# Attention scores in PSUM: the row maxima on a ring of four banks, the scores on two

## The reference, cut to what matters

```
q, k, v = heads(x @ Wq), heads(x @ Wk), heads(x @ Wv)        # 16 heads, D = 32
attn = softmax(q k^T / sqrt(D));  std = (attn v) @ Wo
qa, ka = affinities(q), affinities(k)                        # to 8 splats per head
w = qa amp ka^T;  w = w / (sum_k w + 1e-8);  dgsa = (w v) @ Wo
out = (1 - blend) std + blend dgsa
```

## Time and profile before

| what | value |
|---|---|
| median of 3 runs | 1607.84 us (1604.98 to 1620.33) |
| the profiled execution | 1618.21 us, of which the span of its trace is 1616.0 us |
| mean granted clock of PE | 0.846 of full speed |
| busy: PE, DVE, ACT, POOL | 76%, 75%, 46%, 16% of the span |
| matmul instructions, DVE instructions | 4597, 1425 |

### The profile page before, as it was taken

How to read it: one execution, slowest core, us unless ns; L and a number is a source line. 1 busy time by engine, 2 the same in 40 slices (tenths; PEclk the granted TensorE clock), 3 DMA queues, 4 the chain that set the end, 5 groups by cost and what they waited for, 6 DMA issues and landing times.

```text
span 1616.0 us, 14035 instructions
## 1 busy us (share of the span) xinstructions
PE 1224.5 (76%) x4597; PEld 573.4 (35%) x4602; DVE 1214.8 (75%) x1425; ACT 744.4 (46%) x1102; POOL 257.9 (16%) x299
## 2 busy tenths in 40 slices
PE   5664747777788857788888867778888867786895
PEld 4332212323444422233444422223444422232453
DVE  5968979789648986889547986889648985889423
ACT  6674425443376424444365524444376423443231
POOL 1000222001112221001112231001112221011111
PEclk8766978879899978789799978789799977889798
DMA  6853894655249793555259694555258694455253
GB/s 199 268 165 99 187 217 110 128 118 116 81 119 216 167 225 108 121 114 130 54 132 221 144 220 117 113 121 127 57 134 204 154 216 115 99 127 114 61 141 97
DMA packets 116759, 228.54 MB, mean 141 GB/s; under 512 B 14560, under 2 KB 25312, under 8 KB 116688
## 3 DMA queue, kind: packets, MB, share of 16 engines
q1 hardware_dynamic: 89248, 144.95, 31.6%
q0 software_dynamic: 26496, 81.80, 26.7%
q10 hardware_dynamic: 944, 0.92, 0.2%
HBM read 116.08 MB, written 29.62 MB: 90 GB/s over the span
## 4 chain that ended last, share of the span: by engine, by line
DVE 31%; PE 31%; DMA 14%; issue 7%; ACT 4%; SPq 2%; POOL 1%; DVEq 0%; ACTq 0%; POOLq 0%
PE ps L1420 12%; DVE ST L844 10%; PE ps L1390 6%; DMA qk_parts<-PT 5%; DVE ST L836 5%; DVE MX L900 4%; PE ps L1228 4%; DMA GU<-gu_tiles 4%; PE ps L1245 3%; DVE ST L847 3%; DVE BST L880 2%; DMA KS<-qk_parts 2%; DMA YA<-ST 2%; SPq L343 2%; PE ps L1334 1%
## 5 line engine op out<-in xcount | busy, mean ns | idle before, releaser
L844 DVE TENSOR_TENSOR_SCAN ST<-dA,ST 128x1024 f32<-128x1024 f32 x128 | 316.6, 2473 | 15.3 <-ACT dA L546 11.8
L1420 PE MATMUL ps<-V,GU 128*128 128x512 f16 x1024 | 251.3, 403 | 25.0 <-DMA GU<-gu_tiles 19.4
L1228 PE MATMUL ps<-KS,QS 96*128 96x512 f32 x256 | 135.8, 610 | 149.5 <-DVE MX L900 80.4
L900 DVE TENSOR_REDUCE MX<-ps 128x1 f32<-128x512 f32 x256 | 164.9, 686 | 107.0 <-PE ps L1228 107.0
L447 POOL DMA_DIRECT2D YA<-ST x128 | 109.6, 856 | 819.6 <-DVE ST L847 793.6
L546 ACT ACTIVATE dA<-DL,Aneg 128x511 f32<-128x511 f32 x256 | 168.8, 713 | 95.5 <-DVE ST L844 95.3
L677 ACT ACTIVATE PT<-ps 128x1024 f32<-128x1024 f32 x128 | 125.0, 1019 | 118.7 <-PE ps L1334 118.0
L836 DVE TENSOR_TENSOR ST<-DU,BC 128x1024 f32<-128x1024 f32 x128 | 155.9, 1218 | 12.7 <-DMA BC<-bc_rows 7.9
L847 DVE TENSOR_TENSOR ST<-ST,BC 128x1024 f32<-128x1024 f32 x128 | 159.4, 1245 | 4.4
L1420 PEld LDWEIGHTS ps<-V,GU 128*128 128x128 bf16 x1024 | 100.3, 103 | 169.7 <-issue 42.3
L1390 PE MATMUL ps<-WP,QS 128*128 128x512 f32 x512 | 145.6, 429 | 14.2 <-DVE QS L1033 13.0
(11 more groups left out here) (224 smaller groups left out, 1627.8 us busy)
## 6 DMA issues: line engine op xcount, KB each, us to landing
YA<-ST POOLq DMA_DIRECT2D x128, 512.0 KB, 7.3
BC<-bc_rows SPq DMA_DIRECT2D x64, 512.0 KB, 5.6
qk_parts<-PT SPq DMA_DIRECT2D x64, 256.0 KB, 6.6
GU<-gu_tiles SPq DMA_DIRECT2D x64, 256.0 KB, 3.5
WP<-proj_tiles SPq DMA_DIRECT2D x64, 256.0 KB, 2.8
QS<-qk_parts SPq DMA_DIRECT2D x48, 256.0 KB, 5.3
KS<-qk_parts SPq DMA_DIRECT2D x48, 256.0 KB, 6.0
RD<-PT POOLq DMA_DIRECT2D x28, 256.0 KB, 4.9
```

The lines of the kernel that those rows point to most:

```text
L844: nc.vector.tensor_tensor_scan(flat, dA[:, a, :, :].rearrange("p e s -> p (e s)"), flat, 0.0, ALU.mult, ALU.add).then_inc(s_scan, 1)
L900: nc.vector.tensor_reduce(MX[:, j % 2, qt, h:h + 1], ps[:, n % 2, :], AX_X, ALU.max).then_inc(s_mx, 1)
L1228: mm(ps[:, n % 2, :], QS[i][0:3 * D, h, qt * P:(qt + 1) * P], KS[i][0:3 * D, h, :], start=True, stop=True).then_inc(s_xs, 1)
L1420: last = mm(ps[:, f % F_RING, :], GU[:, t % 2, k, m * P:(m + 1) * P], XHL[:, z, k, :], start=(k == 0 and z == 0), stop=(k == KT - 1 and z ...
```

## The change

Three things move together.

1. The max tiles get a ring of four banks, 0 to 3, from tile n = 20 of each batch on. The first 20 tiles (those of group 0, and the four of group 1 that come ahead of the stage) stay on banks 0 and 1. A tile waits for the reduction of the tile that had its bank before.
2. Both score pairs use banks 4 and 5, so pair s waits for the exponential of pair s - 1. PE's order in a quarter changes with it: before it was pair 0, tiles, pair 1, tiles, values bank 6, tiles, values bank 7, tiles; now it is pair 0, tiles, values bank 6, tiles, pair 1, tiles, values bank 7, tiles. In quarter 0 of groups 1 to 3 no tile stands between the pairs.
3. The splat transposes and the key-value product move to bank 3 (SPARE_BANK). The wait for ACT's copy stands at the first tile of group 2 in bank 3, and the wait for `splat_kv` at the first tile of group 3 in bank 3, which is tile 2 (n = 50). The denominator product moves behind pair 1 of its quarter.

```diff
+        MAX_TILES = KT * HG
+        def max_bank(j, m):
+            n = MAX_TILES * j + m
+            return n % 2 if n < MAX_TILES + X_AHEAD else (n + 1) % 4
+        def max_bank_before(j, m):
+            n = MAX_TILES * j + m
+            same = [q for q in range(n) if max_bank(*divmod(q, MAX_TILES)) == max_bank(j, m)]
+            return same[-1] if same else None
+        def first_in_bank(j, m):
+            return all(max_bank(j, q) != max_bank(j, m) for q in range(m))
+        SPARE_BANK = 3
...
-                        nc.scalar.copy(QAK[:, 2, :], ps[:, 1, :]).then_inc(s_ka, 1)
+                        nc.scalar.copy(QAK[:, 2, :], ps[:, SPARE_BANK, :]).then_inc(s_ka, 1)
...
-                            nc.scalar.activation(PT[:, kt % 2, 2 * p:2 * p + 2, :], ps[:, 2 + 2 * p:4 + 2 * p, :],
+                            nc.scalar.activation(PT[:, kt % 2, 2 * p:2 * p + 2, :], ps[:, 4:6, :],
...
-                    nc.vector.tensor_reduce(MX[:, j % 2, qt, h:h + 1], ps[:, n % 2, :], AX_X, ALU.max).then_inc(s_mx, 1)
+                    nc.vector.tensor_reduce(MX[:, j % 2, qt, h:h + 1], ps[:, max_bank(j, i), :], AX_X, ALU.max).then_inc(s_mx, 1)
...
-                    if n >= 2:
-                        pe.wait_ge(s_mx, 16 * NG * b + n - 1)
-                    if j > 0 and m == 0:
+                    bank, before = max_bank(j, m), max_bank_before(j, m)
+                    if before is not None:
+                        pe.wait_ge(s_mx, 16 * NG * b + before + 1)
+                    if j > 0 and bank == 0 and first_in_bank(j, m):
                         since(pe, s_br, NG * b + j)
-                    if j == 2 and m == 1:
+                    if j == 2 and bank == SPARE_BANK and first_in_bank(j, m):
                         pe.wait_ge(s_ka, b + 1)
-                    mm(ps[:, n % 2, :], QS[i][0:3 * D, h, qt * P:(qt + 1) * P], KS[i][0:3 * D, h, :],
+                    if j == KV_GROUP + 1 and bank == SPARE_BANK and first_in_bank(j, m):
+                        pe.wait_ge(s_kvm, 4 * b + 4)
+                    mm(ps[:, bank, :], QS[i][0:3 * D, h, qt * P:(qt + 1) * P], KS[i][0:3 * D, h, :],
...
-                        steps = (0, 0, 4, 4) if j > 0 and kt == 0 else (0, 2, 4, 6)
+                        steps = (0, 0, 0, 4) if j > 0 and kt == 0 else (0, 2, 4, 6)
                         cuts = [min(tiles[0] + n, tiles[1]) for n in steps] + [tiles[1]]
                         for p in range(2):
                             s = 2 * (KT * j + kt) + p
-                            if s < 2:
+                            if s == 0:
                                 pe.wait_ge(s_dist, 2 * (b + 1))
                                 pe.wait_ge(s_pj2, 2 * (b + 1))
                             else:
-                                pe.wait_ge(s_exp, 2 * KT * NG * b + s - 1)
+                                pe.wait_ge(s_exp, 2 * KT * NG * b + s)
...
-                                last = mm(ps[:, 2 + h, :], KS[i][0:3 * D + 1, h, kt * P:(kt + 1) * P],
+                                last = mm(ps[:, 4 + h % 2, :], KS[i][0:3 * D + 1, h, kt * P:(kt + 1) * P],
...
-                                pe.wait_ge(s_kvm, 4 * b + 4)
-                            max_scores(b, j + 1, cuts[p], cuts[p + 1])
-                        if j == NG - 1 and kt == 0:
-
-                            pe.wait_ge(s_br, NG * (b + 1))
-                            pe.wait_ge(s_kvm, 4 * b + 3)
-                            mm(ps[:, 0, :], QAK[:, 4, 0:P], QAK[:, 0, :], start=True, stop=True).then_inc(s_den, 1)
-                        for p in range(2):
+                            max_scores(b, j + 1, cuts[2 * p], cuts[2 * p + 1])
+                            if j == NG - 1 and kt == 0 and p == 1:
+
+                                pe.wait_ge(s_br, NG * (b + 1))
+                                pe.wait_ge(s_kvm, 4 * b + 3)
+                                mm(ps[:, 0, :], QAK[:, 4, 0:P], QAK[:, 0, :], start=True, stop=True).then_inc(s_den, 1)
                             if kt > 0:
                                 values(b, j, kt - 1, 6 + p)
-                            max_scores(b, j + 1, cuts[2 + p], cuts[3 + p])
+                            max_scores(b, j + 1, cuts[2 * p + 1], cuts[2 * p + 2])
```

More of the change, by code:

```diff
@@ L947, in splat_kv @@
                 dve.wait_ge(s_kv, b + 1)
-                nc.vector.scalar_tensor_tensor(out=QAK[:, 3, :], in0=ps[:, 1, :], scalar=par[:, AMP:AMP + 1], in1=mask,
+                nc.vector.scalar_tensor_tensor(out=QAK[:, 3, :], in0=ps[:, SPARE_BANK, :], scalar=par[:, AMP:AMP + 1], in1=mask,
                                                op0=ALU.mult, op1=ALU.mult).then_inc(s_kvm, 1)
@@ L1340, in attention_phase @@
                                 for k in range(KT):
-                                    last = mm(ps[:, 1, :], QAK[:, 2, k * P:(k + 1) * P], V[:, k, :], start=(k == 0), stop=(k == KT - 1))
+                                    last = mm(ps[:, SPARE_BANK, :], QAK[:, 2, k * P:(k + 1) * P], V[:, k, :],
+                                              start=(k == 0), stop=(k == KT - 1))
                                 last.then_inc(s_kv, 1)
-                                pe.wait_ge(s_kvm, 4 * b + 4)
-                            max_scores(b, j + 1, cuts[p], cuts[p + 1])
-                        if j == NG - 1 and kt == 0:
-                            pe.wait_ge(s_br, NG * (b + 1))
-                            pe.wait_ge(s_kvm, 4 * b + 3)
-                            mm(ps[:, 0, :], QAK[:, 4, 0:P], QAK[:, 0, :], start=True, stop=True).then_inc(s_den, 1)
-                        for p in range(2):
+                            max_scores(b, j + 1, cuts[2 * p], cuts[2 * p + 1])
[3 more added lines that the diff above has]
+                                mm(ps[:, 0, :], QAK[:, 4, 0:P], QAK[:, 0, :], start=True, stop=True).then_inc(s_den, 1)
                             if kt > 0:
                                 values(b, j, kt - 1, 6 + p)
-                            max_scores(b, j + 1, cuts[2 + p], cuts[3 + p])
+                            max_scores(b, j + 1, cuts[2 * p + 1], cuts[2 * p + 2])
                         if j + 1 < NG and kt == KT - 2:
@@ L1366, in attention_phase @@
                         for k in range(KT):
-                            last = nc.tensor.transpose(ps[:, 1, k * P:(k + 1) * P], QAK[:, 1, k * P:(k + 1) * P], ident[:, :])
+                            last = nc.tensor.transpose(ps[:, SPARE_BANK, k * P:(k + 1) * P], QAK[:, 1, k * P:(k + 1) * P], ident[:, :])
                         last.then_inc(s_kat, 1)
```

## The result

The changed kernel took **1632.51 us** (median of 4 runs, 1625.71 to 1637.67), the kernel before on the same chip 1607.19 us (4 runs, 1604.98 to 1620.33). The ratio on record is 1.0128, with a 95% interval of 1.0093 to 1.0164; the quotient of these two medians is a little larger, 1.0158. I had forecast 1604.4 us and a range of 1584 to 1620 us, so the result lies above the range.

What follows compares the result with a forecast made beforehand. A stage was taken as a chain alternating DVE's maxima with PE's tiles and the link through the stack load. Terms -13.4 - 11.6 + 10.4 + 4.1 + 3.6 + 3.45 = -3.5 us gave 1604.4 us, range 1584 to 1620.

Steps and rivals of the forecast that it cites:

- Group 1: Max tiles of group 1: four banks remove 3.35 of DVE's 4.67 us idle time per batch, 13.4 us over four batches.
- Group 2: Max tiles of group 2: four banks remove 2.9 us of DVE's idle time per batch, 11.6 us over four batches.
- rival A: PE's clock rises early in groups 1 and 2 without bank stalls, and costs hide: 1585 us; chance 0.20.
- Load of the stack: Group 0 to 1: the last score pair releases SP's load 2.0 us later; 2.6 us a batch, 10.4 us lost in all.
- From group 1 to 2: Last maximum of group 1 to first of group 2: 14.55 us in the changed kernel, 4.1 us lost in all.
- T0: Start of the transposes, put 0.1 us after the last maximum in the changed kernel.
- Landing: Stack load's DMA time from issue to arrival: taken as 10.3 us, near the lower of 9.73 and 11.74 us.
- Rival B: Stack load bounds: each us of landing beyond 10.3 costs 8 us, giving 1616 to 1624 us; chance 0.14.
- Hidden behind DVE's three halves: Group 3: some 0.7 us more per quarter on ACT and PE costs nothing; only the late denominator costs, 3.45 us.
- Group 0: Score pairs no longer run ahead, so tile 8 reaches DVE late: 0.9 us, 3.6 us lost in all.
- the splat product is late: Group 1 to 2: DVE gets `splat_kv` at 13.1 us where ready at 11.4, hidden unless the landing takes under 9.5 us.
- what would show it: Profile signs: DVE's idle time falls from 107.0 to about 80 us, with 4.5 to 5 us ahead of group 1's first maximum.

Runs made afterwards that it cites:

- experiment 5: Changed kernel, but in the last quarter of groups 0 and 1 POOL issues the YA additions only after the stack load has landed; 1615.56 us, ratio 1.0029.
- experiment 6: Changed kernel, but SP issues the last quarter's BC loads in groups 0 and 1 only after the stack has landed; 1629.29 us, ratio 1.0112.
- experiment 4: Kernel before, but SP issues the stack load only after the group's last exponential has ended; 1645.3 us, ratio 1.0214.
- Experiment 2: Changed kernel, but all of group 3 has pair 1 on banks 2 and 3 and the old PE order; 1624.86 us, ratio 1.0082.
- experiment 1: Changed kernel, but the last quarter of groups 0 to 2 has pair 1 on banks 2 and 3 and the old order; 1593.34 us, ratio 0.9878.
- experiment 11: Kernel before, with only the last quarter's score pairs moved ahead of the transposes; 1599.63 us, ratio 0.9932.
- experiment 10: Kernel before's banks, new PE order in quarters 1 and 2 of groups 1 and 2, last quarter's score pairs ahead of the transposes; 1592.86 us, ratio 0.9903.
- experiment 7: Changed kernel, with the max tiles of all groups back on banks 0 and 1; 1662.75 us, ratio 1.0312.
- experiment 9: Kernel before's banks, with only the new PE order in quarters 1 and 2 of groups 1 and 2; 1606.7 us, ratio 0.9961.

## Why the prediction was wrong

**The gains were right or too small.** Group 1 gained 13.9 us for 13.4, by the walk that I had made: the halves of quarter 1 start 10.4 us after the landing (1036.93 against 1026.56 us), forecast 10.3, and quarter 2 has no gap. Group 2 gained 21.1 us for 11.6. The term was mis-sized because I walked through it at the clock of before; it was granted 0.86 to 0.95. This is rival A's mechanism, in one of its two groups. Group 1 stayed at 0.64 to 0.69. The Trainium skill ("TensorE: Matmul & The Clock Gate", "A second HAM failure mode: psum-queue depth-cycling") reports of another kernel that its clock went up and down as it cycled through PSUM banks. Here the ring of four is in place in both groups, and the clock was no lower than before in either (0.64 to 0.69 for 0.58 to 0.68 in group 1).

**The step that failed is "Load of the stack"**, and with it the term "From group 1 to 2". I forecast 14.5 us for both ways together and they cost 37.3. (The four differences behind the 4.1 us add up to 4.0.) Split by the eight loads, 20.9 us are later issues and 16.2 us slower landings (0.2 are left).

- *Issue.* I took 2.0 us more per load and it was 2.6, up to 3.6 in group 0. I had the last pair end at T0 + 3.65 us, in every load, with a pair's duration at the full clock. Two things held it up. In group 0 of batches 1 to 3 it was ACT's order: I had ended the first exponential at T0 + 3.1 us, from the ACT rows of the old order. With one pair at a time, quarter 2's last exponential ended later; the four dA exponentials of the next halves and the bias row stand behind it in ACT's order, and the exponential that releases the last pair stands behind those (the chain above). It ended at T0 + 3.9 (1014.40 against 1010.52 us), and SP issued 4.7 to 5.2 us after T0. In the other five loads ACT stood idle ahead of the bias row, so its order held nothing. In three of those (group 0 of batch 0, group 1 of batches 2 and 3) PE had the low clock there, 0.50 to 0.56, and SP issued 4.6 to 4.9 us after T0; in the last two, at a clock of 0.96 and 1.00, 3.8 to 3.9 us, near the forecast. Batch 2, group 1 (T0 is 1045.37 us, the issue 1050.29 us):

```profile
1046.42 0.58 ACT L613 ACTIVATE XD<-ps 4x512 fp32r<-4x512 f32 x1 [1.91 <-PE ps L1255]
```

```profile
1045.40:1050.30 4.90, 4.90 (x20) 1.68 (x24) 4.83 (x4) 1.61 (x3) 0.00 (x0) 0.50 0.39 74
```

  A step that is moved moves what stands behind it on its engine; I had counted PE's queue that way and not ACT's.
- *Landing.* I took 10.3 us since seven of eight loads of before were near it, and it was 12.2 (11.4 to 14.2). The eighth load, 11.74 us, I had as an outlier, and it was one of the three that stood closest to the addition. In the trace of before, the five loads that started 3.3 to 3.4 us ahead of the next YA addition landed after 9.6 to 10.2 us, the three that started 2.2 to 2.4 us ahead of it after 9.6, 10.4 and 11.7. In the changed kernel the two starts lie at most 1.2 us apart. I named this neighbour and still took the value of the loads that had the distance. Experiments 5 and 6 show that the addition is the cause and the BC loads are not, and experiment 4 that a late issue alone makes the landing slow as well.

Rival B was therefore the right one. I had ended its price at 1624, at a landing of 12.7 us, since I had the issue 0.6 us per load too early and took group 3's loss for a third of what it was.

**"Hidden behind DVE's three halves" failed for group 3.** It lost 11.7 us for 3.45. `splat_normalise` came 1.3 to 2.2 us later in each batch, 6.9 in all, and from there to the last `normalise` another 1.2 us each, 4.8 in all. The 0.7 us per quarter on ACT and PE add up to the inverse of the sums, and DVE waits for that now:

```profile
1109.02 0.69 DVE L924 TENSOR_TENSOR X<-ps,RD 128x512 f32<-128x512 f32 x1 [0.97 <-ACT RD L634]
```

Experiment 2 gave back 7.4 us of group 3's 11.7. I had seen that the inverse would be "ready just before DVE needs it": with no slack left, each error in the steps ahead is paid in full. Group 0 cost 6.0 us for 3.6: 1.1 to 1.4 us in three batches, but 2.4 us in batch 0.

**Right, besides:** the splat product is late, its wait hides behind the landing (3.06 us for `splat_kv`, then still 2.07 for the tiles), and shows when the landing is short, as in experiment 5. **Wrong in what would show it:** DVE's idle time did not fall to 80 us, since what left the stretches came back ahead of the first maxima, which in group 1 wait 7.5 to 10.3 us where I had put 4.5 to 5. In the kernel of experiment 1, which has the ring without the late load, it is 80.3 us:

```profile
L920 DVE TENSOR_REDUCE MX<-ps 128x1 f32<-128x512 f32 x256 | 160.9, 683 | 80.3 <-PE ps L1249 80.3
```

**Left open.** The 4.6 us between two kernels that are alike in group 0 show how much one profile can be off: there the clock is 1.00 in some batches and about 0.7 in others, for a reason that no run showed. Why group 2 got the high clock and group 1, with the same order and the same ring, did not, was not settled either. The new order and the ring are not the whole of it, since experiment 11, with neither, was granted 0.81 there. In group 2 the tiles begin with ten in one burst where group 1 begins with four, which no run varied by itself.

## What to carry to other kernels

When banks are moved from one pair of engines to another, ask first which release at the end of a stage starts a transfer. Here score pairs confined to two banks cost most in one quarter of four, where the last pair releases the stack load. With that quarter left as it was, the same ring is 1.2% faster than the kernel before; kept to the places where it pays, and with the scores ahead of the transposes, 2.4%. Some 1.0% of that comes without any ring, from the order and the moved transposes (experiment 10).

A DMA's landing time from the trace holds for its neighbours in time. Before taking it for a transfer that moves, look at what is issued next to its new start, and take the one outlier of the old trace for what it shows.

## What the runs showed of the hardware

- The stack load (six DMAs) landed in 9.4 to 10.2 us with the YA addition held back, and in 11.4 to 14.2 us when that was issued between 0.2 us ahead of its first DMA and 1.2 us behind it. SP's own issues in such a load took up to 1.73 us each; in most the first ones took at most 0.43 us.
- The same tile stretch of group 0 in the kernel before took 14.87 us in two batches at a granted clock of 1.00 and 17.57 us in one at 0.71, with the same 24 DVE instructions in all.
- In the tile stretch of group 2 the granted clock rose from 0.68 to 0.70 (19.7 to 20.2 us long) to 0.86 to 0.95 (14.4 to 15.4 us) with the new banks and order. With the order on two banks it was 0.75 to 0.95 (experiment 7) and, with no pair held back, 0.69 to 0.86 (experiment 9); with neither order nor banks but the scores ahead of the transposes 0.81 to 0.82 (experiment 11). So none of the parts is shown to be the cause.
